# Cross keys of a decoder layer projected once for each pair of heads and doubled by transfers within SBUF

## What is computed

```python
x = x + _L0_attn_ref(_layernorm(x), ...)          # one head of 256, scores (q A) q^T / 16
x = x + _L0_xattn_ref(_layernorm(x), ctx, mask)   # 4 heads of 64
x = x + _L0_ffn_ref(_layernorm(x), ...)           # the best of 4 experts for each row

# the cross attention
q = (x @ Wq).reshape(B, N, H, D).transpose(0, 2, 1, 3)
kv = (context @ Wkv).reshape(B, M, 2, H, D).transpose(2, 0, 3, 1, 4)
k, v = (kv[0], kv[1])
attn = jnp.einsum('bhnd,bhmd->bhnm', q, k) * SCALE
attn = jax.nn.softmax(jnp.where(mask[:, None, :, :], attn, -jnp.inf), axis=-1)
out = jnp.einsum('bhnm,bhmd->bhnd', attn, v).transpose(0, 2, 1, 3).reshape(B, N, C) @ Wo
```

## Time and profile before

| | |
|---|---|
| three runs | 825.9, 829.59, 830.28 us; median 829.59 |
| profiled execution | 825.48 us, of which the span is 823.7 |
| PE busy | 747.4 us, 91% |
| DVE, ACT, POOL busy | 628.6, 458.3, 165.7 us |
| first part (before the first tile) | 0 to about 95 us |
| tiles | about 95 to 665 us |
| experts | from about 680 us |

### The profile page before, as it was taken

How to read it: one execution, slowest core, us unless ns; L and a number is a source line. 1 busy time by engine, 2 the same in 40 slices (tenths; PEclk the granted TensorE clock), 3 DMA queues, 4 the chain that set the end, 5 groups by cost and what they waited for, 6 DMA issues and landing times. The chain is left out here.

```text
span 823.7 us, 19809 instructions
## 1 busy us (share of the span) xinstructions
PE 747.4 (91%) x6136; PEld 671.9 (82%) x6137; DVE 628.6 (76%) x1608; ACT 458.3 (56%) x930; POOL 165.7 (20%) x254
## 2 busy tenths in 40 slices
PE   3888889999999999999999999999997735999996
PEld 2778779889888898888988989889896624999996
DVE  4984747888888888888888888888886754777773
ACT  2554536666666666666666666666665612444342
POOL 3100130212303123031230311303112011222221
PEclk9999989999999999999999999999999967999999
DMA  6233233314123141231312314223169381111110
GB/s 218 72 101 112 74 132 109 102 39 133 65 75 106 38 131 64 74 106 38 131 66 72 106 38 131 71 67 106 38 238 413 112 315 27 37 40 40 39 33 15
DMA packets 51142, 80.88 MB, mean 98 GB/s; under 512 B 4894, under 2 KB 29216, under 8 KB 50976
## 3 DMA queue, kind: packets, MB, share of 16 engines
q1 hardware_dynamic: 49232, 75.63, 27.3%
q0 software_dynamic: 1872, 4.76, 1.6%
HBM read 45.60 MB, written 35.18 MB: 98 GB/s over the span
## 5 line engine op out<-in xcount | busy, mean ns | idle before, releaser
L1127 ACT ACTIVATE ps_cross<-flip 128x512 f16<-128x512 f32 (+1 forms) x256 | 124.8, 515 | 109.9 <-PE flip L846 88.9
L1352 DVE TENSOR_TENSOR ps_cross<-flip,ps_cross 128x512 f16<-128x512 f32 (+1 forms) x256 | 144.9, 584 | 30.0 <-ACT ps_cross L1127 28.5
L1313 ACT ACTIVATE exp_cross<-exp_cross,xneg 128x1024 f32<-128x1024 f32 (+1 forms) x128 | 122.7, 960 | 28.1 <-DVE xneg L1512 28.1
L846 PE MATMUL flip<-ident,exp_cross 128*128 128x128 f32 (+1 forms) x832 | 130.0, 279 | 7.0 <-DVE ps_cross L1352 3.6
L835 PE MATMUL scores<-keys_cross,qt 128*128 128x402 f32 x512 | 125.8, 367 | 3.9 <-DVE xneg L1512 2.1
L723 PE MATMUL scores<-keys_self,u_tile 128*128 128x512 f32 x384 | 102.4, 403 | 6.4 <-issue 4.7
L846 PEld LDWEIGHTS flip<-ident,exp_cross 128*128 128x128 f32 (+1 forms) x832 | 94.3, 141 | 14.8 <-DVE ps_cross L1352 5.1
L822 PE MATMUL flip<-vals_self,ps_self 128*128 128x256 f32 x768 | 103.2, 288 | 0.0
L857 PE MATMUL cross_out<-vals_cross,ps_cross 128*128 128x128 f16 (+1 forms) x832 | 100.8, 222 | 0.9 <-DVE ps_cross L1352 0.9
L822 PEld LDWEIGHTS flip<-vals_self,ps_self 128*128 128x128 f32 x768 | 96.3, 193 | 0.1
L859 PE MATMUL cross_out<-vals_cross,ps_cross 128*128 128x64 f16 (+1 forms) x832 | 94.1, 194 | 0.0
(11 more groups left out here) (197 smaller groups left out, 1187.3 us busy)
## 6 DMA issues: line engine op xcount, KB each, us to landing
rows_dram<-pads SPq DMA_DIRECT2D x17, 520.0 KB, 3.9
w_piece<-W SPq DMA_DIRECT2D x32, 256.0 KB, 2.9
w_dram<-w_high SPq DMA_DIRECT2D x32, 256.0 KB, 2.3
w_dram<-w_piece SPq DMA_DIRECT2D x32, 256.0 KB, 2.7
w1s<-w_dram SPq DMA_DIRECT2D x8, 1024.0 KB, 13.1
w2s<-w_dram SPq DMA_DIRECT2D x8, 1024.0 KB, 11.8
u_dram<-u_out SPq DMA_DIRECT2D x4, 1024.0 KB, 5.8
u_tile<-u_dram SPq DMA_DIRECT2D x16, 256.0 KB, 2.7
```

The lines of the kernel that those rows point to most:

```text
L846: tr = pe.transpose(flip[0:rows, bank(use), n * P:(n + 1) * P], exp_cross[:, h % 2, m * P:m * P + rows], ident[:, :])
L1127: return act.activation(out, in_, ACT.Copy, **kw)
L1313: act.activation(exp_cross[:, h % 2, cols], exp_cross[:, h % 2, cols], ACT.Exp, bias=xneg[:, h % 2, 1:2], scale=-1.0, accum_out=xden[:, ha ...
L1352: return dve.tensor_tensor(out, full, hi, ALU.subtract)
```

## The change

The weights of the keys are held once (`wk_cross`). PE projects two heads at a time: head 2p lands in partitions 0 to 63, head 2p + 1 in 64 to 127, of bank n % 4 for step n = 2g + pair, eight steps in all. ACT and DVE write both parts of both heads to slot 2p of `keys_cross`. SP then moves the odd head from partitions 64 to 127 of slot 2p to both halves of slot 2p + 1 (`odd_keys`, two DMAs a step), and when all 16 of these have landed copies the even head from partitions 0 to 63 to 64 to 127 of its slot (`even_keys`, four DMAs). PE waits for `keys_doubled` in the second tile, ahead of the first cross scores.

The maximum of the values is taken by thirteen reductions, one for each piece as soon as it is copied, before the keys. The scale follows the second low part in place of the eighth, and the values' two parts follow the key steps from the third on, with the last five pieces behind the eighth key step.

```diff
@@ -177,12 +177,12 @@
     pro2 = ExitStack()
     w2_raw = sb("w2_raw", [P, 4, C, D], F32, pro2)
-    wk_dup = sb("wk_dup", [P, 2, C, H, 2, HD], F32R, pro2)
+    wk_cross = sb("wk_cross", [P, 2, C, D], F32R, pro2)
     wv_cross = sb("wv_cross", [P, 2, C, D], F32R, pro2)
     ctx_raw = sb("ctx_raw", [P, C, KB], F32, pro2)
     ctx_t = sb("ctx_t", [P, 2, C, MP], F32R, pro2)
     v_f32 = sb("v_f32", [P, MC, D], F32, pro2)
-    v_max = sb("v_max", [P, 2, 4], F32, pro2)
+    v_max = sb("v_max", [P, 2, MC], F32, pro2)
     v_top = sb("v_top", [P, 2], F32, pro2)
     pro2.close()
@@ -458,6 +460,17 @@
         store_u(GROUPS - 1)
         sp.wait_ge(u_stored, 16 * GROUPS)
         sp.wait_ge(cross_w_lo, 4)
+
+        def odd_keys(n):
+            sp.wait_ge(cross_k_hi, n + 1)
+            sp.wait_ge(cross_k_lo, n + 1)
+            cols, h = slice((n // 2) * KB, (n // 2 + 1) * KB), 2 * (n % 2)
+            for half in (slice(HD, P), slice(0, HD)):
+                sp.dma_start(keys_cross[half, :, h + 1, cols].bitcast(F32), keys_cross[HD:P, :, h, cols].bitcast(F32)).then_inc(odd_keys_set, 16)
+
+        def even_keys(h):
+            for part in range(2):
+                sp.dma_start(keys_cross[HD:P, part, h, :].bitcast(F32), keys_cross[0:HD, part, h, :].bitcast(F32)).then_inc(keys_doubled, 16)
         def loads_a(t):
             sp.dma_start(u_tile[:, :, :].bitcast(F32), u_dram[bass.ds(t, 1), :, :, :].rearrange("a p c s -> p (a c) s")).then_inc(u_loaded, 16)
@@ -493,6 +506,11 @@
         loads_a(0)
         loads_x(0)
+        for n in range(8):
+            odd_keys(n)
+        sp.wait_ge(odd_keys_set, 16 * 16)
+        even_keys(0)
+        even_keys(2)
         sp.wait_ge(prologue_done, 3)
         loads_m(0)
@@ -618,7 +636,7 @@
             pool.tensor_tensor(rstd_pro[:, cols], var_eps[:, cols], minus_half[:, cols], ALU.pow).then_inc(pro_powers, 1)
             pool.tensor_tensor(std_pro[:, cols], mv_pro[:, cols, 1], plus_half[:, cols], ALU.pow).then_inc(pro_powers, 1)
-        pool.wait_ge(v_max_part, 4)
+        pool.wait_ge(v_max_part, MC)
         pool.partition_all_reduce(v_max[:, 1, :], v_max[:, 0, :], P, bass.bass_isa.ReduceOp.max).then_inc(v_pool_step, 1)
         pool.wait_ge(prologue_done, 3)
@@ -782,18 +800,19 @@
             three(flip[0:rows, m % 2, 0:D], lambda a, c: ctx_t[:, a, c, m * P:m * P + rows],
                   lambda b, c: wv_cross[:, b, c, :]).then_inc(cross_v_ready, 1)
         for g in range(4):
-            for h in range(H):
-                if g:
-                    pe.wait_ge(cross_k_lo, H * (g - 1) + h + 1)
-                elif h < 2:
+            for pair in range(2):
+                n = 2 * g + pair
+                if n >= 4:
+                    pe.wait_ge(cross_k_lo, n - 3)
+                elif n < 2:
                     pe.wait_ge(pro_q_lo, C * GROUPS)
                 else:
                     pe.wait_ge(pro_v_biased, 4 * GROUPS)
-                three(scores[:, h, 0:KB], lambda a, c: wk_dup[:, a, c, h, :, :],
+                three(scores[:, n % 4, 0:KB], lambda a, c: wk_cross[:, a, c, pair * P:(pair + 1) * P],
                       lambda b, c: ctx_t[:, b, c, g * KB:(g + 1) * KB]).then_inc(cross_k_ready, 1)
-        pe.wait_ge(cross_k_lo, 4 * H)
+        pe.wait_ge(cross_k_lo, 8)
         def self_scores(j, k, n):
             if n == 0:
@@ -825,6 +844,8 @@
         def cross_scores(j, k, h, half):
             if h == 0 and half == 0:
+                if k == 1:
+                    pe.wait_ge(keys_doubled, 16 * 4)
                 pe.wait_ge(qt_ready, j)
             if h == 0 and k < T:
                 pe.wait_ge(self_exp, 2 * j + half + 1)
@@ -1163,9 +1184,7 @@
             if g == 0:
                 act.wait_ge(cross_w_loaded, 64)
-                for dup in range(2):
-                    copy(wk_dup[:, 0, :, :, dup, :], w2_raw[:, 0, :, :].rearrange("p c (h d) -> p c h d", h=H)).then_inc(cross_w_hi, 1)
-                for n, w in ((1, wv_cross), (2, wq_cross), (3, wo_cross)):
+                for n, w in ((0, wk_cross), (1, wv_cross), (2, wq_cross), (3, wo_cross)):
                     copy(w[:, 0, :, :], w2_raw[:, n, :, :]).then_inc(cross_w_hi, 1)
             act.wait_ge(ctx_loaded, 16 * (g + 1))
             act.wait_ge(v_scale_step, 1)
@@ -1181,15 +1200,19 @@
         act.wait_ge(u_stored, 16 * GROUPS)
         act.wait_ge(u_lo_ready, C * GROUPS)
         act.wait_ge(pro_v_lo, 4 * GROUPS)
-        for g in range(4):
-            for h in range(H):
-                act.wait_ge(cross_k_ready, H * g + h + 1)
-                copy(keys_cross[:, 0, h, g * KB:(g + 1) * KB], scores[:, h, 0:KB]).then_inc(cross_k_hi, 1)
-                if g >= 2:
-                    for m in value_chunks(H * (g - 2) + h):
-                        act.wait_ge(v_scale_step, 4)
-                        act.activation(vals_cross[:, m, :, 0, :], v_f32[:, m, :].rearrange("p (h d) -> p h d", h=H), ACT.Copy,
-                                       scale=v_scale[:, 0:1]).then_inc(cross_v_hi, 1)
+        def values_hi(n):
+            for m in value_chunks(n):
+                act.wait_ge(v_scale_step, 4)
+                act.activation(vals_cross[:, m, :, 0, :], v_f32[:, m, :].rearrange("p (h d) -> p h d", h=H), ACT.Copy,
+                               scale=v_scale[:, 0:1]).then_inc(cross_v_hi, 1)
+
+        for n in range(8):
+            act.wait_ge(cross_k_ready, n + 1)
+            copy(keys_cross[:, 0, 2 * (n % 2), (n // 2) * KB:(n // 2 + 1) * KB], scores[:, n % 4, 0:KB]).then_inc(cross_k_hi, 1)
+            if n >= 2:
+                values_hi(n - 2)
+        values_hi(6)
+        values_hi(7)
         copy(barrier[:, 0:1], ident[:, 0:1]).then_inc(prologue_done, 1)
         act.wait_ge(prologue_done, 3)
@@ -1434,16 +1457,11 @@
             u_lo(g)
             if g == 0:
-                for dup in range(2):
-                    dve.wait_ge(cross_w_hi, dup + 1)
-                    for c in range(C):
-                        op = low(wk_dup[:, 1, c, :, dup, :], w2_raw[:, 0, c, :].rearrange("p (h d) -> p h d", h=H),
-                                 wk_dup[:, 0, c, :, dup, :].bitcast(F32))
-                    if dup:
-                        op.then_inc(cross_w_lo, 1)
+                dve.wait_ge(cross_w_hi, 1)
+                low(wk_cross[:, 1, :, :], w2_raw[:, 0, :, :], wk_cross[:, 0, :, :].bitcast(F32)).then_inc(cross_w_lo, 1)
             if g == 1:
                 for n, w in ((1, wv_cross), (2, wq_cross), (3, wo_cross)):
-                    dve.wait_ge(cross_w_hi, 2 + n)
+                    dve.wait_ge(cross_w_hi, 1 + n)
                     low(w[:, 1, :, :], w2_raw[:, n, :, :], w[:, 0, :, :].bitcast(F32)).then_inc(cross_w_lo, 1)
             dve.wait_ge(ctx_hi, g + 1)
             cols = slice(g * KB, min((g + 1) * KB, M))
@@ -1451,34 +1469,38 @@
+        for m in range(MC):
+            dve.wait_ge(cross_v_copied, m + 1)
+            dve.tensor_reduce(v_max[:, 0, m:m + 1], v_f32[:, m, :], AX.X, ALU.max, apply_absolute_value=True).then_inc(v_max_part, 1)
+
+        def values_lo(n):
+            for m in value_chunks(n):
+                dve.wait_ge(cross_v_hi, m + 1)
+                dve.wait_ge(v_scale_step, 4)
+                dve.scalar_tensor_tensor(out=vals_cross[:, m, :, 1, :], in0=v_f32[:, m, :].rearrange("p (h d) -> p h d", h=H),
+                                         scalar=v_scale[:, 0:1], in1=vals_cross[:, m, :, 0, :], op0=ALU.mult,
+                                         op1=ALU.subtract).then_inc(cross_v_lo, 1)
+
         dve.wait_ge(u_stored, 16 * GROUPS)
-        for g in range(4):
-            for h in range(H):
-                if g == 0:
-
-                    dve.wait_ge(cross_v_copied, MC)
-                    dve.tensor_reduce(v_max[:, 0, h:h + 1], v_f32[:, MC * h // H:MC * (h + 1) // H, :], AX.XY, ALU.max,
-                                      apply_absolute_value=True).then_inc(v_max_part, 1)
-                dve.wait_ge(cross_k_hi, H * g + h + 1)
-                cols = slice(g * KB, (g + 1) * KB)
-                low(keys_cross[:, 1, h, cols], scores[:, h, 0:KB], keys_cross[:, 0, h, cols].bitcast(F32)).then_inc(cross_k_lo, 1)
-                if g == 1 and h == H - 1:
-                    dve.wait_ge(v_pool_step, 2)
-                    dve.tensor_reduce(v_top[:, 0:1], v_max[:, 1, :], AX.X, ALU.max).then_inc(v_top_ready, 1)
-                    dve.wait_ge(v_top_ready, 1)
-                    dve.tensor_scalar(v_top[:, 1:2], v_top[:, 0:1], 1e-30, 1.0 / V_TOP, ALU.max, ALU.mult).then_inc(v_scale_step, 1)
-                    dve.wait_ge(v_scale_step, 2)
-                    dve.tensor_copy(v_scale[:, 1:2], v_top[:, 1:2]).then_inc(v_scale_step, 1)
-                    dve.reciprocal(v_scale[:, 0:1], v_top[:, 1:2]).then_inc(v_scale_step, 1)
-                if g >= 2:
-                    for m in value_chunks(H * (g - 2) + h):
-                        dve.wait_ge(cross_v_hi, m + 1)
-                        dve.wait_ge(v_scale_step, 4)
```

(24 more changed lines are left out.)

## The result

| | before | changed |
|---|---|---|
| median of 6 runs, us | 829.25 (825.9 to 832.33) | **840.03** (838.02 to 840.83) |
| ratio, 95% interval | | **1.0134** (1.0106 to 1.0162) |
| profiled execution, us (span) | 825.48 (823.7) | 839.36 (837.6) |
| mean granted clock of the span | 0.975 | 0.953 |

The account below looks back on a forecast made before the run. PE was busy for 91%, but the first tile starts by the landing of w_piece, at 101.4 us; behind the transfers it lands at 106.9, so +5.5 us on the 829.6 median gives 835.1 us, range 823.5 to 840.0.

Parts of the forecast that it names:

- the 8.9 us of PE: Key projection at the prologue's end: 48 matmuls go, taking 8 x 1.11 = 8.9 us off PE.
- The rate: Twenty transfers within SBUF on SP's queue: about 205 GB/s, half of the full queue's 400 to 420.
- The ceiling of the gain: Prologue's end: prologue_done 8.4 us sooner, the whole gain if nothing else stood in between.
- The rate's reason: Transfers: half rate because bytes pass SBUF's side twice and all sixteen reads are from the same 64 partitions.
- rival 1: Transfers at the full rate, 410 GB/s: w_piece lands at 95.8, -5.6 us, 824.0 us; chance 0.20.
- the term L: Landing of w_piece, which starts the first tile: from 101.4 to 106.9 us, +5.5 us.
- PE starts at 75.33 - 0.7 = 74.6.: Start of the key projection: 0.7 us sooner, since DVE's work on the weights is shorter.
- Issued by 99: SP's queue: mask and w_piece issued by 99 us, standing right behind the four large transfers.
- I take the same cost: PE's half clock after the idle wait: same cost as before, -1 to +2 us left in the range.
- the forecast's own case: Half rate, give or take a tenth: +3.5 to +9 us, 832 to 840 us; chance 0.55.
- Rival 3: Eight small transfers writing the partitions they read drop to 103 GB/s: w_piece lands at 115, 843 us; chance 0.07.
- Rival 4: w_piece lands ahead of the transfers, at 93 to 98, 821 to 826 us; counted with rival 1, together 0.20.

Follow-up runs that it names:

- max_only: Kernel before with only the thirteen piecewise reductions for the values' maximum in place of its four; 828.64 us, ratio 0.9997.
- no_transfers: Changed kernel without its twenty transfers and the wait for them, so the attention's values differ from the reference's; 820.58 us, ratio 0.9894.
- wide: Changed kernel with the same number of transfers and bytes within keys_cross, each over all 128 partitions; 828.26 us, ratio 0.9986.
- crossing: Changed kernel with one of each step's two transfers reading partitions 0 to 63 rather than 64 to 127; 836.81 us in a single run.
- direct_late: As direct, but SP issues the last four steps' eight transfers behind mask and w_piece; 824.96 us, ratio 0.9939.
- best: As direct_late, with the first tile's exponentials on ACT ahead of the copy of w_piece; 824.64 us, ratio 0.994.
- best2: As best, with PE's first scores waiting for low parts one by one and the second tile's u_tile ahead of the late transfers; 822.03 us, ratio 0.9929.
- direct: Changed kernel with ACT and DVE writing both heads' slots in one instruction, 16 transfers for the wrong halves, no second stage; 824.99 us, ratio 0.9942.
- piece_first: Changed kernel with SP issuing mask and w_piece ahead of the wait for the sixteen small transfers and the four large ones; 829.4 us, ratio 0.9997.
- base_bank_exp: Control for best2: kernel before, with first scores waiting bank by bank and first tile's exponentials ahead of w_high; 829.19 us, ratio 0.9999.
- act_queue: Changed kernel with the first two w_piece loads issued from ACT's own queue behind prologue_done, not from SP; 826.08 us, ratio 0.9953.

## Why the prediction was wrong in its size

**Right.** What waits for what: the first tile starts by the landing of `w_piece`, the twenty transfers stand ahead of it in SP's queue, and the 8.9 us of PE end in a longer wait of ACT. The projection lasts 8.99 us. The rate: 205 GB/s forecast, 185 to 206 measured; the packets of the large transfers took 8.2 us, 8.0 forecast. The maximum costs nothing (max_only), the all-reduce took 0.44 us for thirteen columns, PE does not wait for `keys_doubled`, the tiles keep their pace. The ceiling of the gain, 8.4 us, was 8.8 in no_transfers.

**Half right.** The rate's reason. Two were given; wide shows that the half of the partitions is the whole of it. The Trainium skill, SBUF — State Buffer, section "Door 1: The DMA port swizzle", states that rule; the traces agree, at 206 GB/s against 381 to 409 over all partitions, but in crossing a queue of such transfers in alternating directions went above its limit of 218 GB/s, to 221 to 241 in most slices, and there the measurement decides. The Trainium skill's page that gave rival 1 (DMA: Bandwidth & Descriptors, "Where 436 GB/s comes from": a copy within SBUF is bound by the fabric's 435 GB/s) agrees with wide alone; for the transfers of this change it is twice too high.

**Wrong: the term L**, 106.9 forecast, 111.5 measured. Here it is taken apart by its events:

| | forecast | measured | miss |
|---|---|---|---|
| first transfer issued | at 77.2 | at 78.13 | +0.9 |
| from there to its first packets | 1.0 | 1.4 | +0.4 |
| packets of the small ones and the pads | 17.3 | 18.3 | +1.0 |
| from there to SP's next issue | 0.4 | 0.75 | +0.35 |
| from there to the first packets of the large ones | 0.7 | 1.2 | +0.5 |
| packets of the large ones (99.7 to 107.9) | 8.0 | 8.2 | +0.2 |
| from there to L, the start of `w_high` | 2.3 | 3.6 | +1.3 |

So 2.5 of the 4.6 us are issue and landing, 1.2 the packets (a rate near 200 rather than 205, and the pads), 0.9 a late start. The first and last packets of the small ones stand in the changed kernel's DMA views of 78 to 80 and of 97 to 99 us, in slices of 0.05 us (the two lone slices before 79.5 are instruction fetches):

```profile
GB/s 0 0 0 0 0 0 0 0 0 0 0 0 0 0 0 164 0 0 0 0 0 0 0 328 0 0 0 0 0 0 225 129 193 289 64 257 193 64 354 64
```

```profile
GB/s 193 161 129 161 161 129 97 161 32 161 64 64 64 32 0 64 0 0 0 0 0 0 0 0 0 0 0 0 0 0 0 0 0 0 0 0 0 0 0 0
```

1. *"PE starts at 75.33 - 0.7 = 74.6."* It started at 75.49. A lead was there before it, 1.2 us, but PE then ran at a lower clock. The timelines show the values' projection of before (first row) and of the change (second):

```profile
67.04 8.45 PE L723 MATMUL flip<-wv_cross,ctx_t 128*128 128x256 f32 x66 [3.05 <-ACT v_f L1127]
```

```profile
65.81 9.85 PE L741 MATMUL flip<-wv_cross,ctx_t 128*128 128x256 f32 x66 [3.00 <-ACT v_f L1148]
```

The same 66 matmuls took 9.85 us rather than 8.45. The granted clock of 65 to 70 was 0.67, part of it at 1.2 GHz, and 1.00 before, after nearly the same idle time (3.00 and 3.05 us). The clock took the lead back, and the first transfer went out at 78.13, 0.9 us late. In direct_late, which had no half clock at this place, the projection started at 73.83. How much of the lead is the weights' is not shown: max_only, with the old weights, starts the values' projection at 65.86.

2. *"Issued by 99"* for the mask and `w_piece`. They were issued at 103.08, 105.05 and 107.09. I had given each issue the 0.33 to 0.43 us of the earlier trace rows, but with a full queue SP's issues took 0.98 us (median of the sixteen) and up to 1.99: SP issued at the pace at which the engines drained. A load that was to stand right behind the transfers was therefore issued only when these had almost gone, and its landing (4.4 us after the issue, median) could not lie wholly beside them. This also let `u_tile` (0.26 MB, issued at 107.63) run beside the second piece. Both are in the last row of the table, at most 1.3 us; no run separates them.

3. *"I take the same cost"* for the half clock behind the long wait. In the change the last stretch at 0.50 ends at 121.3 us, 7.6 us after PE's restart, before it ended 6.1 us after; and the second tile fell into another, 134.9 to 138.3. I put on it the 0.7 us between the exponential's shift and that of `x1`, and the 1.1 of the second tile. For the latter the other traces speak too: in no_transfers, wide, crossing, direct_late, best and best2, which have half clock in the second tile as well, its `x1` falls back by 1.1 to 2.4 us against the first tile's; in direct, piece_first and max_only, which have none there, by 0.1 us at most.

The range had +2 us for the clock and a tenth for the rate, but nothing for issue and landing, which alone came to 2.5 us. With +9 as its upper edge the forecast's own case had no room for what happened.

**Rival 3** (a quarter of the rate where a transfer writes the partitions it reads), at 843, was nearer in time and is wrong: half of the bytes at 103 GB/s would have given slices near 137, and they show 185 to 206. A near number is no evidence for a mechanism. **Rival 4** was excluded rightly by program order; piece_first shows what undoing that order gives.

## What to carry to other kernels

Work taken from the bounding engine of a stretch and given to a DMA queue is not free if the hand-over to the next stretch hangs on a load in that queue: price it by what stands behind it there, count SP's issues at the queue's pace when the queue is full, and allow for issue and landing at each wait of the chain. And look at the second hand-over as well: in base_bank_exp and act_queue the first tile was 4 us early and the second was not. Here three loads in another place of one queue were worth 10.6 us (piece_first), more than the projection's whole gain. Transfers within SBUF between partition halves should be as few as the producing engine can make them by writing twice, and go in both directions side by side.

## What the runs showed of the hardware

- Transfers of 64 partitions within SBUF: 185 to 206 GB/s where all sources lie in one half, 208 to 279 where two directions alternate (crossing, direct), 381 to 409 over 128 partitions with rows of 3.2 KB (wide).
- An issue on SP took 0.33 to 0.43 us with an idle queue, 0.59 at the least for a transfer of 64 x 2 rows, and 0.98 (median) to 1.99 us behind transfers that filled the engines, in the changed kernel.
- A load from a second queue gets through: 5.5 us from issue to landing on ACT's queue amid SP's transfers, 4.4 us on SP's when they had almost gone.
- ACT and DVE, 804 columns out of 402 in PSUM: 0.83 and 0.99 us, where 402 columns took 0.51 and 0.58.
- At the same place of the program, where PE comes back from 2.7 to 3.1 us of idle time to the values' projection, the clock is at 1.2 GHz for a while in ten of the thirteen traces, and at 2.4 GHz throughout in three (before, base_bank_exp, direct_late); what decides it is open.
